# Shifting the key and value weights of a cross-attention kernel by 32 bytes within the SBUF partition

## What is computed

```python
def xattn(query, key, value, mask, Wq, bq, Wk, bk, Wv, bv, Wo, bo):   # key = value = context, 2 x 8192 x 512
    q, k, v = query @ Wq.T + bq, key @ Wk.T + bk, value @ Wv.T + bv
    att = einsum('bhqd,bhkd->bhqk', heads(q), heads(k)) / sqrt(32)     # 16 heads
    out = einsum('bhqk,bhkd->bhqd', softmax(where(mask == 0, -inf, att)), heads(v))
    return merge(out) @ Wo.T + bo

x = x + xattn(layernorm(x), ctx, ctx, mask, ...)
x = x + windowed_attention(layernorm(x), ...)
x = x + experts(layernorm(x), ...)
```

## The kernel before

| tile | before | modulo 64 / 128 | after | modulo 64 / 128 |
|---|---|---|---|---|
| WKH | 77632 | 0 / 64 | 77664 | 32 / 96 |
| WKL | 85824 | 0 / 64 | 85856 | 32 / 96 |
| WVH | 94016 | 0 / 64 | 94048 | 32 / 96 |
| WVL | 102208 | 0 / 64 | 102240 | 32 / 96 |
| bv_s | 110464 | 0 / 0 | 110496 | 32 / 32 |
| XN | 112512 | 0 / 0 | 112544 | 32 / 32 |
| CH0 | 143712 | 32 / 96 | 143776 | 32 / 32 |
| CL0 | 160096 | 32 / 96 | 160160 | 32 / 32 |
| KS0, QS0 (attention) | 59200, 67392 | 0 / 64 | the same | 0 / 64 |
| WH0, XEH0 (experts) | 108768, 182496 | 32 / 96 | the same | 32 / 96 |

## Time and profile before

### The profile page before, as it was taken

How to read it: one execution, slowest core, us unless ns; L and a number is a source line. 1 busy time by engine, 2 the same in 40 slices (tenths; PEclk the granted TensorE clock), 3 DMA queues, 4 the chain that set the end, 5 groups by cost and what they waited for, 6 DMA issues and landing times. The chain is left out here.

```text
span 2841.6 us, 37454 instructions
## 1 busy us (share of the span) xinstructions
PE 2804.9 (99%) x14165; PEld 1767.7 (62%) x14165; DVE 2171.4 (76%) x1600; ACT 1721.9 (61%) x2488; POOL 87.8 (3%) x43
## 2 busy tenths in 40 slices
PE   8999999999999999999999999999999999999998
PEld 5888888888744444444444444445554688888886
DVE  5544444444399999999999999946547888889886
ACT  4122211122299999999999999724531477777775
POOL 0000000000000000000000000000000300000000
PEclk9999999999999999999999999999999999999999
DMA  6555555555555555555555565321120699999995
GB/s 217 181 190 193 177 197 186 177 193 191 183 135 138 133 134 135 134 132 140 128 143 138 130 141 125 90 73 45 45 110 35 232 376 349 344 351 343 343 350 197
DMA packets 229105, 515.51 MB, mean 181 GB/s; under 512 B 18131, under 2 KB 84051, under 8 KB 199629
## 3 DMA queue, kind: packets, MB, share of 16 engines
q1 hardware_dynamic: 225372, 505.15, 56.5%
q0 software_dynamic: 3584, 8.39, 1.3%
HBM read 400.03 MB, written 113.44 MB: 181 GB/s over the span
## 5 line engine op out<-in xcount | busy, mean ns | idle before, releaser
L861 DVE TENSOR_TENSOR AC<-AC,PR 128x2048 f32<-128x2048 f32 x448 | 988.5, 2283 | 5.2 <-ACT PR L825 5.2
L825 ACT ACTIVATE PR<-PS 128x512 f32<-128x512 f32 x1024 | 567.7, 610 | 54.2 <-PE PS L746 42.1
L746 PEld LDWEIGHTS PS<-QS,KS 128*128 128x128 f32 x2048 | 364.9, 188 | 339.7 <-ACT PR L829 182.3
L746 PE MATMUL PS<-QS,KS 128*128 128x512 f32 x2048 | 564.2, 416 | 6.5 <-PEq L535 6.1
L829 ACT ACTIVATE PR<-PS 128x1024 f32<-128x1024 f32 x512 | 502.3, 1051 | 0.0
L757 PE MATMUL PS<-PR,VC 128*32 128x512 f32 x4096 | 492.5, 598 | 0.7 <-ACT PR L825 0.7
L912 DVE TENSOR_TENSOR WL<-RAW,WH 128x2048 fp32r<-128x2048 f32 x192 | 436.4, 2287 | 59.5 <-ACT WH L907 59.5
L392 ACT ACTIVATE KH<-PS,bk_s 128x512 fp32r<-128x512 f32 x128 | 87.8, 688 | 556.6 <-PE PS L446 556.6
L907 ACT ACTIVATE WH<-RAW 128x2048 fp32r<-128x2048 f32 x192 | 362.0, 1913 | 10.6 <-PE PS L1346 5.2
L289 DVE SCALAR_TENSOR_TENSOR KL<-PS,bk_s,KH 128x512 fp32r<-128x512 f32 x128 | 95.5, 750 | 268.8 <-ACT KH L392 268.8
L757 PEld LDWEIGHTS PS<-PR,VC 128*32 128x32 f32 x4096 | 106.8, 109 | 216.3 <-issue 170.9
(11 more groups left out here) (207 smaller groups left out, 3215.9 us busy)
## 6 DMA issues: line engine op xcount, KB each, us to landing
KS<-kh_d SPq DMA_DIRECT2D x256, 256.0 KB
RAW<-in_gw SPq DMA_DIRECT2D x64, 1024.0 KB, 5.3
RAW<-in_up_w SPq DMA_DIRECT2D x64, 1024.0 KB
RAW<-in_down_w SPq DMA_DIRECT2D x64, 1024.0 KB, 5.1
kh_d<-KH SPq DMA_DIRECT2D x32, 1024.0 KB, 4.4
kl_d<-KL SPq DMA_DIRECT2D x32, 1024.0 KB, 6.5
v_d<-VS SPq DMA_DIRECT2D x128, 256.0 KB, 2.9
KS<-kl_d SPq DMA_DIRECT2D x128, 256.0 KB
```

The source lines that it names most:

```text
L746: pe.matmul(PS[:, m % RING, :], KS[N % 2][:, j, t * P:(t + 1) * P], QS[bg % 2][:, j, :], start=True, stop=True).then_inc(s_s, 1)
L825: nc.scalar.activation(PR[tile % BUFS][:, 2 * hp + jj], PS[:, bank + jj, :], ACT.Exp, scale=SCALE).then_inc(s_exp, 1)
L861: v.tensor_tensor(a[i % 2][:], a[i % 2][:], p[:], ALU.add).then_inc(s_acc, 1)
```

## The change

A tile `LINE` of 8 floats (32 bytes) per partition, which nothing reads or writes, is declared ahead of `WKH`, and `ln_tmp`, declared behind `XN`, grows from 15 to 16 floats for each of 8 tiles: 480 to 512 bytes. Tiles from `WKH` to `ln_tmp` begin 32 bytes later, those behind it 64 bytes later. No instruction is added, removed or moved on any engine, and the other three blocks keep their addresses.

```diff
             def sb(name, shape, dt=F32):
                 return s1.enter_context(nc.sbuf_tensor(name, shape, dt))
 
+            LINE = sb("LINE", [P, 8])
             WKH, WKL, WVH, WVL = (sb(n, [P, DC, D], F32R) for n in ("WKH", "WKL", "WVH", "WVL"))
             bk_s, bq_s, bv_s = sb("bk_s", [P, G]), sb("bq_s", [P, G]), sb("bv_s", [P, D])
             XN = sb("XN", [P, TT, D])
-            tmp = sb("ln_tmp", [P, TT, 15])
+            tmp = sb("ln_tmp", [P, TT, 16])
             QH, QL = sb("QH", [P, 2, SQ], F32R), sb("QL", [P, 2, SQ], F32R)
```

## The result

| | before | changed |
|---|---|---|
| median | 2845.48 us (20 runs, 2841.35 to 2848.24) | 2840.27 us (20 runs, 2836.41 to 2844.95) |
| ratio | | 0.9985, 95% interval 0.9979 to 0.9991 |
| the profiled execution | 2843.35 us | 2843.58 us |
| its span | 2841.6 us | 2841.8 us |

The ratio is that of the means, 2840.88 over 2845.11 us. By it the change is worth 0.15% of the time, 4.3 us, with an interval from 2.6 to 6.0; the medians lie 5.2 us apart. The forecast was 19.1 us. What came is within the 0.2% that I had called no change.

What follows compares the result with a forecast made beforehand. PE, without gaps in the first block's keys and values, was taken as the bound; 3024 matmuls at 6.3 ns less gave -19.1 us, all other terms nothing, so 2823.5 us, with an 8-in-10 range of 2819 to 2844.

Steps and rivals of the forecast that it cites:

- What bounds the stage, and what is late next: First block's keys and values: PE's matmuls alone set the time, and no other engine takes PE's place after the change.
- rival C: PE's gain is taken back at a seam by DMA or DVE ending a chunk; at most a few us, no chance given.
- The cause of the pitch: Keys and values: 233.3 ns against the experts' 226.9 comes from the two operands' addresses relative to each other.
- rival A: Something other than the address slows the first block's matmuls; pitch stays at 233.3 ns, 2842.4 us; chance 0.07.
- The price of one: Keys' and values' products: each matmul gains 6.3 ns at the experts' settled pitch; 3024 of them, 19.1 us.
- Rival D: The line that counts exceeds 64 bytes: no change, 2842.4 us, chance 0.07; or half the gain, 2833 us, 0.06.
- The running-in: Edges between keys and values: none counted; if one came with every chunk, 0.03 us each, 1 us in all.
- the first chunk: Its keys, 48 matmuls of L473, wait for data; even full effect is 0.3 us, and what follows waits on DVE: nothing.
- XN: Now 32 bytes off; its transposes take 273 ns, those with the experts' HE 272 ns: nothing.
- bv_s: DVE adds it in 686 ns; DVE is busy 301 of 660 us, so even a tenth more would hide: nothing.
- Rival B: 64 apart is the worst position: pitch up to 240 ns, 2863 us, or half of that, 2852 us; chance 0.10.

Runs made afterwards that it cites:

- the kernel with distance 0: Against the kernel before, LINE added and ln_tmp 30 floats: weights' and context's tiles both begin 352 bytes past a multiple of 512; 2821.74 us, ratio 0.9922.
- the one with 128: Against the kernel before, LINE added and ln_tmp 18 floats: context's tiles begin 128 bytes from the weights' modulo 512; 2842.61 us, ratio 0.9997.
- the kernel with all low parts 128 bytes further: Weights' high parts and CH 320 past a multiple of 512, low parts (WKL, WVL, CL) 128 further; one execution, 2836.51 us.
- the kernel with distances 96 and 160: Fillings ahead of CH and CL put even chunks' context tiles 96 bytes from the weights', odd chunks' 160; one execution, 2842.07 us.

## Why the prediction was wrong

**What bounds the stage, and what is late next: right.** PE had no gap in any of the kernels from 80 to 740 us, even where its matmuls came 2.8% faster, and DVE and ACT went on waiting for it. In the kernel with distance 0 the time fell by 20.9 us, and 3024 matmuls at 6.6 ns come to 20.0, so no seam took anything back (rival C).

**The cause of the pitch: right.** Nothing but addresses differs between the kernel with distance 0 and the one with 128, and they are 20.9 us apart. That refutes rival A. The Trainium skill's page "TensorE: Matmul & The Clock Gate", in "Step-by-step: what each phase is for", has the loading of the next weights take nothing from the running matmul. Read as the prediction read it, that no address could matter, this does not hold here: the place of the two operands to each other moved the distance between matmuls from 226.7 to 233.3 ns. The prediction's own picture, a stream that meets the weight load of the next matmul, was theory N, and it failed in the kernel with all low parts 128 bytes further (231.1 ns, not 226.7).

**The step that failed** is "The price of one is not in this trace for these tiles; the nearest row is the experts' settled pitch", taken for all 3024 matmuls. The experts' operands are 0 apart modulo 512, the changed ones 64, and the two are alike modulo 64 only. As far as the runs go, what counts is the distance modulo 256. In place of 6.3 ns for 3024 matmuls the change gave 4.4 ns for 768 of them and nothing for the rest: 3.4 us, and 4.3 with an interval of 2.6 to 6.0 by the means of the runs. Rival D had this, with the addresses that speak for it, and I gave it 0.13 without a row that spoke against it. That keys and values had one pitch though their distances have opposite signs, which I read as a sign for the pair's position to each other, says nothing on the length: 233.3 is what nearly every distance but 0 gives.

**The running-in, the first chunk, XN and bv_s: nothing, as forecast.** The transposes of XN took 273 ns before and after, and the experts' matmuls 389.

**Rival B, slower:** it did not come, though 160 between moving and stationary operand has 234.2 ns, 0.9 above the pitch before; 1.9 would have been needed to be seen.

**The range**, 2819 to 2844, holds the changed kernel's median, 2840.27, but only through its part for no change. Its likeliest part, 2820 to 2828, had 0.70 and does not. That the range holds it is partly luck besides: the kernel before, 2842.44 us in the three runs that the forecast started from, had a median of 2845.48 in the twenty runs of the comparison, outside of the range that was to take in no change.

**Left open:** why at a distance of 64 keys stay at one of two pitches; why exchanging the buffers puts all keys at the faster; and which read of which matmul meets which other, since three simple rules for it (own operands, the next one's weights, either) each failed on a run.

## What to carry to other kernels

Where a stream of float32r matmuls 128x512 with new weights each time is the bound, put the moving tile and the stationary tile at the same place modulo 256 bytes; here a filling of 480 bytes in front of the context's tiles took 0.74% and with both at 352 modulo 512 it was 0.78%, with no instruction added or moved. When a stage is slower than another with the same instructions, look at the addresses, and before copying the fast one's, ask in how many modulos the two would then agree: make them agree in the largest that costs nothing, and test the smaller ones afterwards. The busy share did not show this cost, 660.00 of 660 us in every kernel; the number of matmuls in a window did, 2830 against 2914.

## What the runs showed of the hardware that was not expected

- The pitch of float32r matmuls 128x512 with their own weight load, at the full clock, takes few values: 226.7 ns with distance 0 modulo 256, 233.3 with nearly every other (234.2 with 160), and about 228.9 and 231.1 (a third and two thirds of the way) where only some of the tiles are unlike. A sequence can settle in more than one of them at the same addresses modulo 256: 228.9 and 233.3 at a distance of 64.
- The weight load lasts 188 ns at either pitch. The cost shows in the distance between the starts of the matmuls, and in the own duration of each: 395 to 396 ns on average from 80 to 740 us before, 389 with distance 0.
- The time at the lower clock is not fixed, though the work there is the same: some 11 us in the two windows of the profile before, 20 in those of the changed kernel. In the profile of the kernel with distances 96 and 160 the clock stays at 1.00 from 1900 to 2000 us, with the same gap of 1.3 us. The difference is as large in effect as the whole change, so that the two profiled executions are 0.2 us apart, the wrong way, while 20 runs of each show the saving.
